# Two norms in a row in four stages of a perceiver network: both scale factors from one pass of moments, the once-normed tokens written behind the twice-normed ones

## The chip, the cores and the metric

The kernel runs on one core of one Trainium2 chip. The metric is the device time of one execution in microseconds (us), and the time of a kernel is the median of several executions. The core has TensorE (PE in the rows; its weight loads are PEld), VectorE (DVE), ScalarE (ACT), GpSimd (POOL) and SyncE (SP), which issues nearly all DMAs (SPq is its queue). The engines run their own instruction streams and wait for each other through semaphores.

## What is computed

The reference is a network of twelve sub-layers over 8 x 64 tokens of 512 float32 features, each added to the residual `x`. Before each one `x` is normed without weights. Four of the sub-layers begin by norming their input once more:

```python
def _layernorm(x, axis=-1, eps=1e-05):
    m = jnp.mean(x, axis=axis, keepdims=True)
    v = jnp.var(x, axis=axis, keepdims=True)
    return (x - m) / jnp.sqrt(v + eps)
...
x = x + _L1_xattn_ref(_layernorm(x, axis=-1), ...)   # begins with a layer norm (eps 1e-5), weights pre_g, pre_b
x = x + _L1_attn_ref(_layernorm(x, axis=-1), ...)    # begins with an RMS norm (eps 1e-6), weight rms_w; adds its input at the end
x = x + _L2_attn_ref(_layernorm(x, axis=-1), ...)    # begins with a layer norm (eps 1e-5), weights ln1_g, ln1_b; adds its input
x = x + _L3_attn_ref(_layernorm(x, axis=-1), ...)    # begins with a layer norm (eps 1e-5), weights g1, beta1; adds its input
```

A token that has been normed once has mean 0 and variance v / (v + eps), v being its variance in `x`. A second norm divides by the root of v / (v + eps) + eps2, so that the product of both divisions is one division by the root of v + eps2 * (v + eps), that is of v * (1 + eps2) + eps * eps2. For a mean of 0 the mean square that an RMS norm uses is the variance.

## The kernel before

The program is one list of stages. A stage is a list of blocks: in each block every engine has its own code, and a block ends with a barrier of all engines, so nothing of the next block starts before all of this one's instructions are issued and the engines have met. A DMA that a block has issued can land later, in a later block; whoever needs its data waits for its semaphore.

The 512 tokens lie in SBUF as four tiles of 128 tokens x 512 features (`t` runs over them): `m.x` (x_tokens in the rows) is the residual, `m.y` (normed_tokens) the normed tokens. `m.yT` (normed_features) holds the normed tokens turned to features x tokens, as four chunks (`c`) of 128 x 512, as the matmuls want them.

`normalise` is one block:

- SyncE issues the loads given in `ahead` one after another (L161), from the start of the block.
- VectorE computes moments of the four tiles (BN_STATS, L201, then BN_AGGR, L204) and variance + eps (L211; for the RMS norm L207 to L209). GpSimd raises that to the power -0.5 (L230), for all 4 x 128 tokens in one instruction. VectorE then writes the four normed tiles (L217, RMS L215).
- If `dstT` is given, TensorE turns the tiles with 16 transposes (L239), of which the first four each wait for one tile. ScalarE takes the chunks 0 and 2 out of PSUM, multiplied by `scale` and with `bias` added (L186), VectorE chunks 1 and 3 (L194, for the RMS norm without bias L192). With `vectors` given both first wait until **all** loads sent with that signal have landed: the weights of the norm are among them, but so are the larger weights of the projection behind.

In the four stages two such blocks stand in a row. The first norms `m.x` into `m.y` without `dstT`. The second norms `m.y`, with `dstT`. In L1_xattn and L1_attn the loads are sent in the first block of the two; in L2_attn and L3_attn, where the second block is the beginning of `transformer_layer`, they are sent in the second. L2_attn calls `transformer_layer` twice, and its second layer has one norm there, of the layer's own `m.y`. Behind the second block comes `linear_features`, whose first matmuls (L281) start the projection. `m.y`, the once-normed tokens, is added again at the end of L1_attn and in the attention of both transformer stages; L1_xattn does not use it again.

Of the kernel before, what the change touches and what calls it, by code (L numbers as in the profile page):

```python
# [66 lines left out]
class Machine:  # L67


    def __init__(self, nc, ctx, d):  # L70
# [11 lines left out]
        self.den = self.sb("var_eps", [P, T])  # L82
        self.rstd = self.sb("rstd", [P, T])
        self.slot_x = nc.dram_tensor("slot_inputs", (SLOT_ROWS, D), F32, kind="Internal").ap()
        self.slot_y = nc.dram_tensor("slot_outputs", (SLOT_ROWS, D), F32, kind="Internal").ap()
# [85 lines left out]

def normalise(m, dst, src, eps, rms=False, dstT=None, scale=None, bias=None, ahead=None, vectors=None):

# [4 lines left out]
    with m.block() as block:  # L178
# [18 lines left out]
        @block.vector  # L197
        def _(dve):
            step = Chain(dve, summed)
            for t in range(T):  # L200
                ins = dve.bn_stats(m.stats[:, t, :], src[:, t, :])  # L201
            step(ins)
            for t in range(T):
                ins = dve.bn_aggr(m.mv[:, t, :], m.stats[:, t, :])  # L204
            step(ins)
            if rms:
                step(dve.tensor_tensor(m.den[:], m.mv[:, :, 0], m.mv[:, :, 0], ALU.mult))  # L207
                step(dve.tensor_tensor(m.den[:], m.den[:], m.mv[:, :, 1], ALU.add))
                dve.tensor_scalar(m.den[:], m.den[:], eps, None, ALU.add).then_inc(*ready.up())  # L209
            else:  # L210
                dve.tensor_scalar(m.den[:], m.mv[:, :, 1], eps, None, ALU.add).then_inc(*ready.up())  # L211
            dve.wait_ge(*rooted.at(1))
            for t in range(T):
                if rms:
                    ins = dve.tensor_scalar(dst[:, t, :], src[:, t, :], m.rstd[:, t:t + 1], None, ALU.mult)  # L215
                else:
                    ins = dve.tensor_scalar(dst[:, t, :], src[:, t, :], m.mv[:, t, 0:1], m.rstd[:, t:t + 1],  # L217
                                            ALU.subtract, ALU.mult)
                if dstT is not None:
                    ins.then_inc(*normed.up())  # L220
            if dstT is not None:
                if landed:
                    dve.wait_ge(*landed)
                for c in range(1, C, 2):
                    take(dve, c)

        @block.gpsimd
        def _(pool):
            pool.wait_ge(*ready.at(1))
            pool.tensor_tensor(m.rstd[:], m.den[:], m.minus_half[:], ALU.pow).then_inc(*rooted.up())  # L230

        if dstT is not None:
# [1262 lines left out]
def L1_xattn(m):  # L1495
# [3 lines left out]
    with m.local(qT=[P, C, N], oT=[P, C, N], w=[P, C, D], pre=[P, 2, C], ln=[P, 2, C], rows=[P, 2, D],  # L1499
                 wkb=[P, C, D], wvb=[P, C, D], ctxT=[P, 2, C, SK]) as (qT, oT, w, pre, ln, rows, wkb, wvb, ctxT):  # L1500
        normalise(m, m.y, m.x, 1e-5, ahead=(
             vectors, (pre[:, 0, :], d["L1_xattn_pre_g"]), (pre[:, 1, :], d["L1_xattn_pre_b"]),
             (ln[:, 0, :], d["L1_xattn_ln_g"]), (ln[:, 1, :], d["L1_xattn_ln_b"]),
             (rows[:, 0, :], d["L1_xattn_ln_g_row"].partition_broadcast(P)),
             (rows[:, 1, :], d["L1_xattn_ln_b_row"].partition_broadcast(P)), (w[:], d["L1_xattn_Wq"])))
        normalise(m, m.y, m.y, 1e-5, dstT=m.yT, scale=pre[:, 0, :], bias=pre[:, 1, :], vectors=vectors)
        linear_features(m, [(qT, None, w, m.yT, None, ACT.Identity)], sent=vectors,
# [338 lines left out]

def transformer_layer(m, z, n, ln1, wq, bq, wk, bk, wv, bv, wo, bo, ln2, w1, b1, w2, b2, act, allowed=None, rope=None):

# [4 lines left out]
    with m.local(wa=[P, C, FF], wb=[P, FF // P, D], cols2=[P, 2, C], b1c=[P, FF // P], b2r=[P, D]) as \  # L1853
            (wa, wb, cols2, b1c, b2r):
        with m.local(qT=[P, C, N], kT=[P, C, N], wqo=[P, C, D], wkk=[P, C, D], cols=[P, 6, C],
# [3 lines left out]
            wvv = wb[:, 0:C, :]  # L1859
            normalise(m, n, z, 1e-5, dstT=m.yT, scale=cols[:, 0, :], bias=cols[:, 1, :], vectors=q_sent, ahead=(  # L1860
                q_sent, *[(cols[:, i, :], d[a]) for i, a in enumerate((ln1[0], ln1[1], bq, bk))],
# [77 lines left out]
def L3_attn(m):  # L1939
    normalise(m, m.y, m.x, 1e-5)  # L1940
    g = lambda a: f"L3_attn_{a}"
    with m.local(n=[P, T, D]) as (n,):
        transformer_layer(m, m.y, n, (g("g1"), g("beta1")), g("Wq"), g("bq"), g("Wk"), g("bk"), g("Wv"), g("bv"),
                          g("Wo"), g("bo"), (g("g2"), g("beta2")), g("W1"), g("b1"), g("W2"), g("b2"), ACT.Relu, rope=True)
    add_into(m, m.x, m.x, m.y)
# [426 lines left out]
def L1_attn(m):  # L2372
# [5 lines left out]
    with m.local(pairs=[P, 6, NC, N], va=[P, NC, N], u=[P, NC, N], W=[P, NC, 512], vecs=[P, 8, NC], convw=[P, NC, 4],  # L2378
# [627 lines left out]
```

## Time and profile before

| | |
|---|---|
| median of 3 runs | 4082.79 us (4082.26 to 4084.75) |
| the profiled execution, its own time | 4083.16 us |
| its span in the trace | 4081.4 us |
| TensorE busy | 3317.2 us, 81% of the span |
| VectorE busy | 1285.6 us, 31% |
| ScalarE busy | 730.7 us, 18% |
| GpSimd busy | 137.4 us, 3% |
| mean granted TensorE clock | 0.88 of full speed |

The shares are an average over stages with different limits. The four pairs of norms are short stretches, about 17 us each from the first moments to the first matmul, and in each TensorE stands idle for most of the time. In the timeline rows below a line is one run of equal instructions: start, duration, engine, line, operation, output<-inputs, shape, count, and in brackets how long the engine had been idle before it and what released it.

### The profile page before, as it was taken

What the parts mean: (1) busy time and instruction counts of PE and PEld (TensorE: products, weight loads), DVE (VectorE), ACT (ScalarE), POOL (GpSimd) and SP (SyncE); (2) the same over time, 40 slices, a digit from 0 to 9 for tenths busy, and PEclk for the clock granted to TensorE, in tenths of its full rate; (3) what the DMA queues carried; (4) which work ended last, traced back from release to release, by engine and by line L of the source; (5) the groups of instructions that cost most, each with busy time, mean ns of one, the idle gap of its engine ahead of it and who ended that gap; (6) DMA issues with size and microseconds to landing.
All of it is one profiled execution on the core that took longest, in us unless ns stands there. A gap on an engine that the chain in (4) does not pass through costs nothing. (4 is left out here: it accounts for less than half of the span.)

```text
span 4081.4 us, 42876 instructions
## 1 busy us (share of the span) xinstructions
PE 3317.2 (81%) x16360; PEld 1483.3 (36%) x16360; DVE 1285.6 (31%) x2692; ACT 730.7 (18%) x1187; POOL 137.4 (3%) x141
## 2 busy tenths in 40 slices
PE   7997799966997966679768979698997897667767
PEld 3443433322444422234324444333443443111111
DVE  2554410003445278644423030412444312000001
ACT  2442111001332210010001011011442111122111
POOL 0000010000000021000000000000000100000000
PEclk9997899987998977889888999799998998777776
DMA  3100289982110101121332030494000206999996
GB/s 124 39 28 32 93 341 414 416 333 98 52 62 21 56 21 52 52 83 52 126 119 96 0 133 0 161 413 160 30 31 18 107 11 255 421 421 420 420 420 288
DMA packets 93807, 654.91 MB, mean 160 GB/s; under 512 B 17779, under 2 KB 18548, under 8 KB 29940
## 3 DMA queue, kind: packets, MB, share of 16 engines
q1 hardware_dynamic: 89524, 639.56, 38.9%
q0 software_dynamic: 4160, 13.63, 0.9%
q8 instruction: 87, 1.43, 0.1%
q14 instruction: 36, 0.29, 0.0%
HBM read 643.71 MB, written 9.44 MB: 160 GB/s over the span
## 5 line engine op out<-in xcount | busy, mean ns | idle before, releaser
L475 PE MATMUL banks<-wvb,ctxT 128*128 128x512 f32 x768 | 346.6, 596 | 0.0
L2288 PE MATMUL banks<-wb,h 128*32 128x512 f32 x1024 | 174.2, 797 | 86.3 <-DMA wb<-in_L_ffn_w 45.6
L2277 PE MATMUL banks<-wa,mine 128*32 128x512 f32 x1024 | 191.5, 863 | 61.3 <-DMA wa<-in_L_ffn_w 42.8
L471 PE MATMUL banks<-ctxT,wkb 128*128 128x512 f32 x512 | 230.9, 596 | 3.3 <-PEq L125 3.3
L475 PEld LDWEIGHTS banks<-wvb,ctxT 128*128 128x128 f32 x768 | 139.2, 190 | 162.5 <-issue 153.6
L1296 PE MATMUL banks<-ring,xT 128*64 128x512 f32 x736 | 168.0, 611 | 12.9 <-DMA ring<-in_L_ffn_Wu 7.7
L281 PE MATMUL banks<-normed_features,wa 128*128 128x512 f32 x384 | 170.9, 608 | 3.5 <-PEq L130 3.5
L331 PE MATMUL banks<-wb,h 128*128 128x512 f32 x384 | 165.5, 593 | 3.1 <-PEq L130 3.1
L693 DVE COPY prT<-banks 128x512 f32<-128x512 f32 x160 | 109.5, 685 | 129.8 <-PE banks L545 128.2
L239 PE MATMUL banks<-identity,normed_tokens 128*128 128x128 f32 x160 | 42.9, 425 | 131.3 <-DVE normed_tokens L217 131.3
L593 ACT ACTIVATE pr<-pr,col 128x512 f32<-128x512 f32 x160 | 114.7, 717 | 119.4 <-DVE col L667 119.4
L471 PEld LDWEIGHTS banks<-ctxT,wkb 128*128 128x128 f32 x512 | 92.7, 190 | 111.0 <-issue 99.6
L545 PE MATMUL banks<-identity,pr 128*128 128x128 f32 x640 | 106.0, 291 | 21.6 <-ACT pr L587 8.0
L471 PE MATMUL banks<-extraT,wkb 128*128 128x512 f32 x256 | 116.4, 609 | 1.0 <-ACT extraT L581 1.0
L2692 PE MATMUL banks<-u,qw 128*128 128x512 f32 x192 | 85.2, 607 | 34.0 <-DMA qw<-in_L_attn_Q_W 34.0
L2584 PE MATMUL banks<-quantT,W 128*128 128x512 f32 x128 | 70.4, 702 | 52.2 <-PEq L130 27.7
L281 PEld LDWEIGHTS banks<-normed_features,wa 128*128 128x128 f32 x384 | 74.8, 196 | 98.2 <-issue 98.2
L545 PEld LDWEIGHTS banks<-identity,pr 128*128 128x128 f32 x640 | 78.3, 147 | 85.9 <-issue 59.5
L331 PEld LDWEIGHTS banks<-wb,h 128*128 128x128 f32 x384 | 72.7, 190 | 95.9 <-issue 95.9
L587 ACT ACTIVATE pr<-sc,col 128x512 f32<-128x512 f32 x96 | 69.3, 722 | 197.3 <-DVE col L662 197.3
L1296 PEld LDWEIGHTS banks<-ring,xT 128*64 128x64 f32 x736 | 62.0, 140 | 116.1 <-issue 114.8
L2288 PEld LDWEIGHTS banks<-wb,h 128*32 128x32 f32 x1024 | 29.1, 128 | 205.0 <-DMA wb<-in_L_ffn_w 131.5
(498 smaller groups left out, 4388.1 us busy)
## 6 DMA issues: line engine op xcount, KB each, us to landing
wa<-in_L_ffn_w SPq DMA_DIRECT2D x128, 1024.0 KB, 26.4
wb<-in_L_ffn_w SPq DMA_DIRECT2D x128, 1024.0 KB, 27.6
ring<-in_L_ffn_Wd SPq DMA_DIRECT2D x24, 2048.0 KB, 25.0
ring<-in_L_ffn_Wg SPq DMA_DIRECT2D x23, 2048.0 KB, 18.1
ring<-in_L_ffn_Wu SPq DMA_DIRECT2D x23, 2048.0 KB, 20.0
wa<-in_L_ffn_W SPq DMA_DIRECT2D x32, 1024.0 KB, 12.2
wb<-in_L_ffn_W SPq DMA_DIRECT2D x32, 1024.0 KB, 10.0
ctxT<-in_ctxT SPq DMA_DIRECT2D x24, 1024.0 KB, 4.8
```

What stands on the lines that cost most here:

```text
L281: ins = pe.matmul(m.ps[:, n % 4, :], buf[:, k, mm * P:(mm + 1) * P], srcT[:, k, :], start=(k == 0), stop=(k == kchunks - 1))
L331: ins = pe.matmul(m.ps[:, t, :], srcT[:, k, t * P:(t + 1) * P], buf[:, k, :], start=(k == 0), stop=(k == kchunks - 1))
L471: ins = pe.matmul(ps[:, u % 2, :], wkb[:, k, u * P:(u + 1) * P], (extraT if knorm else ctxT[:, par])[:, k, :], start=(k == 0), stop=(k == ...
L475: ins = pe.matmul(ps[:, u % 2, :], ctxT[:, par, k, r * P:(r + 1) * P], wvb[:, k, :], start=(k == 0), stop=(k == C - 1))
L545: ins = pe.transpose(ps[:, TB[j % 2], k * P:(k + 1) * P], pr[:, j % R, k * P:(k + 1) * P], m.ident[:])
L593: act.activation(pr[:, j % R, :], pr[:, j % R, :], ACT.Copy, scale=col[:, par, j, 3:4])\
L693: dve.tensor_copy(prT[:, j % RP, :, :], ps[:, TB[j % 2], :].rearrange("p (k n) -> p k n", k=KC))\
L1296: ins = pe.matmul(ps[H * side:H * side + H, 2 * kind + half, :], xT[:, p % 2, k, H * own:H * own + H], rows_of(where[(name, slot)], C)[:, ...
L2277: ins = pe.matmul(ps[B4 * q:B4 * q + B4, 0, :], mine[:, odd, k, :], wa[:, odd, k, q * 512:(q + 1) * 512], start=(k == 0), stop=(k == C - 1))
L2288: ins = pe.matmul(ps[B4 * q:B4 * q + B4, 2, :], h[:, Q * n + q, :], wb[:, odd, n, q, :], start=(n == 0), stop=(n == Q - 1))
L2584: return pe.matmul(ps[:, bank, :], sel[:, q % 4, c, :], quantT[:, q // 4, :], start=True, stop=True)
L2692: ins = pe.matmul(ps[:, n % 2 if n < NC else 2 + n - NC, :], qw[:, n % 2, k, :], u[:, k, :], start=(k == 0), stop=(k == NC - 1))
```

## The change

`normalise` gets two new arguments. With `again` (the eps of the second norm) the factor is computed from one pass of moments for both norms together, so the block writes the twice-normed tokens straight from `m.x`. With `once` it also computes the factor of the first norm alone (`den_once`, and a second power on GpSimd into `rstd_once`) and writes the once-normed tokens into that buffer, behind the other four tiles on VectorE and ahead of VectorE's chunks 1 and 3. The first block of each pair goes. L1_xattn gets `again` alone; L1_attn, L3_attn and the first layer of L2_attn get both.

```diff
+def normalise(m, dst, src, eps, dstT=None, scale=None, bias=None, ahead=None, vectors=None, again=None, once=None):
...
-            if rms:
-                step(dve.tensor_tensor(m.den[:], m.mv[:, :, 0], m.mv[:, :, 0], ALU.mult))
-                step(dve.tensor_tensor(m.den[:], m.den[:], m.mv[:, :, 1], ALU.add))
-                dve.tensor_scalar(m.den[:], m.den[:], eps, None, ALU.add).then_inc(*ready.up())
+            if again is not None:
+                dve.tensor_scalar(m.den[:], m.mv[:, :, 1], 1.0 + again, eps * again, ALU.mult, ALU.add).then_inc(*ready.up())
             else:
                 dve.tensor_scalar(m.den[:], m.mv[:, :, 1], eps, None, ALU.add).then_inc(*ready.up())
+            if once is not None:
+                dve.tensor_scalar(m.den_once[:], m.mv[:, :, 1], eps, None, ALU.add).then_inc(*ready.up())
             dve.wait_ge(*rooted.at(1))
             for t in range(T):
...
+                ins = dve.tensor_scalar(dst[:, t, :], src[:, t, :], m.mv[:, t, 0:1], m.rstd[:, t:t + 1],
+                                        ALU.subtract, ALU.mult)
                 if dstT is not None:
                     ins.then_inc(*normed.up())
+            if once is not None:
+                dve.wait_ge(*rooted.at(2))
+                for t in range(T):
+                    dve.tensor_scalar(once[:, t, :], src[:, t, :], m.mv[:, t, 0:1], m.rstd_once[:, t:t + 1],
+                                      ALU.subtract, ALU.mult)
             if dstT is not None:
                 if landed:
                     dve.wait_ge(*landed)
...
         def _(pool):
             pool.wait_ge(*ready.at(1))
             pool.tensor_tensor(m.rstd[:], m.den[:], m.minus_half[:], ALU.pow).then_inc(*rooted.up())
+            if once is not None:
+                pool.wait_ge(*ready.at(2))
+                pool.wait_ge(*rooted.at(1))
+                pool.tensor_tensor(m.rstd_once[:], m.den_once[:], m.minus_half[:], ALU.pow).then_inc(*rooted.up())
...
-        normalise(m, m.y, m.x, 1e-5, ahead=(
+        normalise(m, m.y, m.x, 1e-5, again=1e-5, dstT=m.yT, scale=pre[:, 0, :], bias=pre[:, 1, :], vectors=vectors, ahead=(
...
-        normalise(m, m.y, m.y, 1e-5, dstT=m.yT, scale=pre[:, 0, :], bias=pre[:, 1, :], vectors=vectors)
...
-            normalise(m, n, z, 1e-5, dstT=m.yT, scale=cols[:, 0, :], bias=cols[:, 1, :], vectors=q_sent, ahead=(
+            twice = {} if before is None else {"again": 1e-5, "once": z}
+            normalise(m, n, z if before is None else before, 1e-5, **twice, dstT=m.yT, scale=cols[:, 0, :], bias=cols[:, 1, :],
+                      vectors=q_sent, ahead=(
...
 def L2_attn(m):
-    normalise(m, m.y, m.x, 1e-5)
...
-                              allowed="strided")
+                              allowed="strided", before=None if i else m.x)
...
 def L3_attn(m):
-    normalise(m, m.y, m.x, 1e-5)
...
-        normalise(m, m.y, m.x, 1e-5, ahead=(
+        normalise(m, rms_normed, m.x, 1e-5, again=1e-6, once=m.y, dstT=m.yT, scale=rmsw[:], vectors=vectors, ahead=(
...
-        normalise(m, rms_normed, m.y, 1e-6, rms=True, dstT=m.yT, scale=rmsw[:], vectors=vectors)
```

On VectorE the start of L1_attn reads so before (`pairs` holds the RMS-normed tokens, L130 is the end of a block):

```order
L201 BN_STATS stats<-x_tokens 128x6 x4
L204 BN_AGGR mean_var<-stats 128x2 x4
L211 TENSOR_SCALAR var_eps<-mean_var 128x4
L217 TENSOR_SCALAR normed_tokens<-x_tokens,mean_var,rstd 128x512 x4
L130 UNCONDITIONAL_BRANCH
L197 UNCONDITIONAL_BRANCH
L201 BN_STATS stats<-normed_tokens 128x6 x4
L204 BN_AGGR mean_var<-stats 128x2 x4
L207 TENSOR_TENSOR var_eps<-mean_var 128x4
L208 TENSOR_TENSOR var_eps<-var_eps,mean_var 128x4
L209 TENSOR_SCALAR var_eps<-var_eps 128x4
L215 TENSOR_SCALAR pairs<-normed_tokens,rstd 128x512 x4
L192 TENSOR_SCALAR normed_features<-banks,rmsw 128x512 x2
```

And so with the change, at the same place on VectorE:

```order
L207 BN_STATS stats<-x_tokens 128x6 x4
L210 BN_AGGR mean_var<-stats 128x2 x4
L213 TENSOR_SCALAR var_eps<-mean_var 128x4
L217 TENSOR_SCALAR var_eps_once<-mean_var 128x4
L220 TENSOR_SCALAR pairs<-x_tokens,mean_var,rstd 128x512 x4
L227 TENSOR_SCALAR normed_tokens<-x_tokens,mean_var,rstd_once 128x512 x4
L198 TENSOR_SCALAR normed_features<-banks,rmsw 128x512 x2
```

One set of moments and one barrier are gone, the writing of normed_tokens stands behind that of pairs instead of ahead of it, and it now stands between pairs and the two chunks that VectorE takes from PSUM.

On GpSimd the start of L2_attn reads so before (L740 is the first instruction of the attention's own block):

```order
L130 UNCONDITIONAL_BRANCH
L227 UNCONDITIONAL_BRANCH
L230 TENSOR_TENSOR rstd<-var_eps,minus_half 128x4
L130 UNCONDITIONAL_BRANCH
L227 UNCONDITIONAL_BRANCH
L230 TENSOR_TENSOR rstd<-var_eps,minus_half 128x4
L130 UNCONDITIONAL_BRANCH
L737 UNCONDITIONAL_BRANCH
L740 MEMSET v 128x64
```

With the change:

```order
L132 UNCONDITIONAL_BRANCH
L235 UNCONDITIONAL_BRANCH
L238 TENSOR_TENSOR rstd<-var_eps,minus_half 128x4
L242 TENSOR_TENSOR rstd_once<-var_eps_once,minus_half 128x4
L132 UNCONDITIONAL_BRANCH
L749 UNCONDITIONAL_BRANCH
L752 MEMSET v 128x64
```

The number of powers stays at two, but the second now stands in the same block and runs while VectorE writes tiles; before, VectorE waited during both.

## Rows read from the trace of the kernel before

**Rows 1.** Timeline at the start of L1_xattn.

```profile
920.99 2.47 DVE L201 BATCH_NORM_STATS2 stats<-x_tokens 128x6 f32<-128x512 f32 x4 [0.55 <-PEq L130]
...
923.70 0.43 SPq L161 DMA_DIRECT2D w<-in_L_xattn_Wq  x1
...
927.47 2.47 DVE L201 BATCH_NORM_STATS2 stats<-normed_tokens 128x6 f32<-128x512 f32 x4 [0.30 <-PEq L130]
...
934.23 0.78 ACT L186 ACTIVATE normed_features<-banks,pre 128x512 f32<-128x512 f32 x1 [33.69 <-PE banks L239]
...
937.84 10.35 PE L281 MATMUL banks<-normed_features,w 128*128 128x512 f32 x19 [1.15 <-PEq L130]
```

**Rows 2.** Timeline at the start of L1_attn.

```profile
1313.98 2.47 DVE L201 BATCH_NORM_STATS2 stats<-x_tokens 128x6 f32<-128x512 f32 x4 [0.30 <-PEq L130]
...
1317.77 0.47 SPq L161 DMA_DIRECT2D convw<-in_L_attn_conv_w  x1
...
1320.41 2.47 DVE L201 BATCH_NORM_STATS2 stats<-normed_tokens 128x6 f32<-128x512 f32 x4 [0.30 <-PEq L130]
...
1327.32 0.69 ACT L186 ACTIVATE normed_features<-banks,rmsw 128x512 f32<-128x512 f32 x1 [14.43 <-PE banks L239]
...
1330.87 14.39 PE L281 MATMUL banks<-normed_features,W 128*128 128x512 f32 x29 [1.09 <-PEq L130]
```

**Rows 3.** Timeline at the start of L2_attn.

```profile
2114.88 2.47 DVE L201 BATCH_NORM_STATS2 stats<-x_tokens 128x6 f32<-128x512 f32 x4 [0.30 <-PEq L130]
...
2121.31 2.47 DVE L201 BATCH_NORM_STATS2 stats<-normed_tokens 128x6 f32<-128x512 f32 x4 [0.30 <-PEq L130]
...
2125.52 1.92 DVE L217 TENSOR_SCALAR n<-normed_tokens,mean_var,rstd 128x512 f32<-128x512 f32 x4 [1.12 <-POOL rstd L230]
...
2126.12 4.03 PE L239 MATMUL banks<-identity,n 128*128 128x128 f32 x16 [12.27 <-DVE n L217]
...
2129.61 1.53 DVE L194 TENSOR_SCALAR normed_features<-banks,cols 128x512 f32<-128x512 f32 x2 [2.17 <-DMA bound<-in_strided]
...
2131.44 13.97 PE L281 MATMUL banks<-normed_features,wqo 128*128 128x512 f32 x32 [1.29 <-PEq L130]
```

**Rows 4.** Timeline at the start of L3_attn.

```profile
3146.72 2.47 DVE L201 BATCH_NORM_STATS2 stats<-x_tokens 128x6 f32<-128x512 f32 x4 [0.30 <-PEq L130]
...
3153.14 2.47 DVE L201 BATCH_NORM_STATS2 stats<-normed_tokens 128x6 f32<-128x512 f32 x4 [0.30 <-PEq L130]
...
3157.96 4.41 PE L239 MATMUL banks<-identity,n 128*128 128x128 f32 x16 [12.27 <-DVE n L217]
...
3162.03 1.53 DVE L194 TENSOR_SCALAR normed_features<-banks,cols 128x512 f32<-128x512 f32 x2 [2.75 <-DMA trig<-in_rope_trig]
...
3163.86 11.38 PE L281 MATMUL banks<-normed_features,wqo 128*128 128x512 f32 x22 [1.49 <-PEq L130]
```

**Rows 5.** DMA issues: size, and us from issue to landing.

```profile
w<-in_L_xattn_Wq SPq DMA_DIRECT2D x1, 1024.0 KB, 7.2
...
convw<-in_L_attn_conv_w SPq DMA_DIRECT2D x1, 16.0 KB, 5.8
```

**Rows 6.** Timeline of L3_attn's rotation: GpSimd beside VectorE, then VectorE alone.

```profile
3200.46 5.83 POOL L1902 TENSOR_TENSOR kT<-kT,trig 128x512 f32<-128x512 f32 x4
3202.12 5.33 DVE L1913 TENSOR_TENSOR qT<-qT,tmp 128x512 f32<-128x512 f32 x4
3207.37 1.28 DVE L1913 TENSOR_TENSOR kT<-kT,tmp 128x512 f32<-128x512 f32 x2
```

**Rows 7.** Windows: us, busy time per engine, granted clock, DMA share, GB/s.

```profile
940.00:942.00 2.00, 2.00 (x3) 0.69 (x3) 0.00 (x0) 0.00 (x0) 0.00 (x0) 0.55 1.01 426
...
1334.00:1336.00 2.00, 2.00 (x5) 0.76 (x4) 0.00 (x0) 0.00 (x0) 0.00 (x0) 0.92 1.00 426
2128.00:2130.00 2.00, 2.00 (x12) 1.91 (x10) 0.39 (x1) 0.40 (x1) 0.00 (x0) 0.59 0.49 166
3166.00:3168.00 2.00, 2.00 (x4) 0.75 (x4) 0.00 (x0) 0.00 (x0) 0.00 (x0) 0.68 1.02 430
```

More of the change, by code:

```diff
@@ L83, in __init__ @@
         self.rstd = self.sb("rstd", [P, T])
+        self.den_once = self.sb("var_eps_once", [P, T])
+        self.rstd_once = self.sb("rstd_once", [P, T])
         self.slot_x = nc.dram_tensor("slot_inputs", (SLOT_ROWS, D), F32, kind="Internal").ap()
@@ L169, in _ @@
             start_loads(sp, ahead)
-def normalise(m, dst, src, eps, rms=False, dstT=None, scale=None, bias=None, ahead=None, vectors=None):
+def normalise(m, dst, src, eps, dstT=None, scale=None, bias=None, ahead=None, vectors=None, again=None, once=None):
     summed, ready, rooted = m.sig("moments_step"), m.sig("variance_ready"), m.sig("rstd_ready")
@@ L205, in _ @@
             step(ins)
-            if rms:
-                step(dve.tensor_tensor(m.den[:], m.mv[:, :, 0], m.mv[:, :, 0], ALU.mult))
-                step(dve.tensor_tensor(m.den[:], m.den[:], m.mv[:, :, 1], ALU.add))
-                dve.tensor_scalar(m.den[:], m.den[:], eps, None, ALU.add).then_inc(*ready.up())
+            if again is not None:
+                dve.tensor_scalar(m.den[:], m.mv[:, :, 1], 1.0 + again, eps * again, ALU.mult, ALU.add).then_inc(*ready.up())
             else:
                 dve.tensor_scalar(m.den[:], m.mv[:, :, 1], eps, None, ALU.add).then_inc(*ready.up())
+            if once is not None:
+                dve.tensor_scalar(m.den_once[:], m.mv[:, :, 1], eps, None, ALU.add).then_inc(*ready.up())
             dve.wait_ge(*rooted.at(1))
             for t in range(T):
[L214 to L218, printed above, removed]
+                ins = dve.tensor_scalar(dst[:, t, :], src[:, t, :], m.mv[:, t, 0:1], m.rstd[:, t:t + 1],
+                                        ALU.subtract, ALU.mult)
                 if dstT is not None:
                     ins.then_inc(*normed.up())
+            if once is not None:
[3 more added lines that the diff above has]
+                                      ALU.subtract, ALU.mult)
             if dstT is not None:
@@ L1844, in L2_xattn, with transformer_layer @@
         linear_tokens(m, m.x, m.yT, None, w, C, bv[:], m.x, sent=vectors)
-def transformer_layer(m, z, n, ln1, wq, bq, wk, bk, wv, bv, wo, bo, ln2, w1, b1, w2, b2, act, allowed=None, rope=None):
+def transformer_layer(m, z, n, ln1, wq, bq, wk, bk, wv, bv, wo, bo, ln2, w1, b1, w2, b2, act, allowed=None, before=None, rope=None):
     d = m.d
@@ L1943, in L3_attn @@
         transformer_layer(m, m.y, n, (g("g1"), g("beta1")), g("Wq"), g("bq"), g("Wk"), g("bk"), g("Wv"), g("bv"),
-                          g("Wo"), g("bo"), (g("g2"), g("beta2")), g("W1"), g("b1"), g("W2"), g("b2"), ACT.Relu, rope=True)
+                          g("Wo"), g("bo"), (g("g2"), g("beta2")), g("W1"), g("b1"), g("W2"), g("b2"), ACT.Relu, rope=True,
+                          before=m.x)
     add_into(m, m.x, m.x, m.y)
```

## The prediction, made before the changed kernel ran

> **What bounds the kernel now.** I read the page first: TensorE is busy 81% of the span and no other engine over 31% (table above), so time is won where TensorE stands idle. The timeline of the four places that the change touches comes next. In each the reader should see the same chain: moments, variance, a wait for GpSimd's power, four tiles, a barrier, then all of it once more, then transposes, chunks taken out of PSUM, a barrier, the first matmul of the projection. TensorE has nothing to do from the end of the stage before to the transposes; in L2_attn that is 12.27 us of idleness [rows 3]. From the first moments to the first matmul it is 937.84 - 920.99 = 16.85 us in L1_xattn, 16.89 in L1_attn, 16.56 in L2_attn and 17.14 in L3_attn [rows 1 to 4].
>
> The third view is what releases the chunks. In L1_xattn and L1_attn ScalarE's first chunk waits for TensorE [rows 1, 2]; in L2_attn and L3_attn VectorE's chunks wait for a DMA, the last small load of the list (bound, trig) [rows 3, 4]. So the pairs are of two kinds. Where the loads were sent in the first of two blocks they have time to land behind the second norm; where they are sent in the second they already end last. The change treats the kinds differently, and this is where the sum is decided.
>
> **L2_attn and L3_attn.** What goes is the first block entire: from first moments to first moments 2121.31 - 2114.88 = 6.43 us and 3153.14 - 3146.72 = 6.42 us [rows 3, 4]. The loads are at the start of the block that stays, so they move ahead by the same time, and the stretch behind them stays as long as it is: in L2_attn chunks at +8.30 us after the moments began, first matmul at +10.13; in L3_attn +8.89 and +10.72. No load of the stage was sent in the block that goes, so nothing loses cover.
>
> What is added on VectorE must end before the chunks. The fused tiles start at 2125.52 - 2121.31 = +4.21 and take 1.92 us, to +6.13; the four once-normed tiles have the same form, another 1.92, to +8.05, say +8.1 with the semaphore. The DMA lands at +8.30 in L2_attn: hidden with 0.2 us to spare. In L3_attn 0.8 us are spare. The new variance (4 columns) lies in VectorE's 1.12 us wait for the power. The second power starts when the first has ended, at about +4.2, and by that same wait takes at most 1.1: ready at +5.3, 0.8 ahead of the fused tiles' end. If the landing were no cover, the added tiles would cost 1.9 us in a stage.
>
> One small loss in L2_attn: its 16 transposes took 4.03 us because the clock rose inside them (0.59 in a window that would read 0.50 at half clock [rows 7]); those of L3_attn took 4.41 [rows 4]. Started at +4.81, 4.41 would end them at +9.22, against VectorE's second chunk at +9.07. I take 0.2 us as lost. Sum: 6.43 - 0.2 + 6.42 = 12.65 us.
>
> **L1_xattn.** Here `ahead` stays in the block that stays, so the loads do not move, while the norm is ready earlier. ScalarE's first chunk came 934.23 - 927.47 = 6.76 us after the second moments began; from 920.99 that is 927.75. But the weight w, last of the list, is issued at 923.70 and lands 7.2 us later, at 930.90 [rows 1, 5]. Both engines wait for all loads, so the chunks start at 930.9: the landing that was hidden behind the second norm now ends last, and eats 3.15 us. From there to the first matmul I take the stretch of L2_attn, where chunks also waited for a DMA: 2131.44 - 2129.61 = 1.83 us. First matmul at 932.73 instead of 937.84: 5.1 us.
>
> **L1_attn.** The last load, convw, is issued at 1317.77 and lands 5.8 us later, at 1323.57 [rows 2, 5]. The norm alone would allow the first chunk at 1313.98 + (1327.32 - 1320.41) = 1320.89, and earlier by the two small VectorE steps that the RMS norm no longer has. The landing ends last again, 2.7 us late. First matmul at 1323.57 + 1.83 = 1325.40 instead of 1330.87: 5.45 us. The once-normed tiles end at about 1313.98 + 8.1 = 1322.1, 1.5 us ahead of the landing: free. They are read again only in the last block of the stage.
>
> **The second power beside VectorE.** Before, VectorE waited during every power. Now one runs while VectorE writes tiles. The trace shows that the two can slow each other: four of VectorE's additions took 5.33 us beside GpSimd's products, 1.33 each, and two more took 1.28 without, 0.64 each [rows 6]. Those are whole tiles; the power has 4 columns. From below the price is nothing. From above one engine waits out the other: VectorE's fused tiles, and the transposes with them, up to 1.0 us late, which costs 1.0 in L2_attn, about 0.6 in L3_attn (chunks there have 0.4 to spare), and some 0.3 in L1_attn; or the power is held until the fused tiles end at +6.13 and the once-normed tiles run from +7.2 to +9.1, 0.8 late in L2_attn and 0.2 in L3_attn. I take nothing, since the one instruction is small against the rows that show the slowing, and keep 2 us for the range.
>
> The Trainium skill speaks against me here: "SBUF — State Buffer", section "Who interferes with whom", has VectorE's tensor_scalar among the operations that can take the port pair shared with GpSimd, for a whole instruction, the other engine blocking fully. By that rule the held power is the case, and the sum would be 1.0 us smaller. Rows 6 agree that the two engines wait for each other, but show it for additions of two inputs.
>
> **The clock.** The granted clock is half (1.2 GHz) when the transposes begin, and what it costs is the matmuls at half clock behind them. In the window from 940 it reads 0.55, that is 0.2 of 2 us at full clock: it rose at 941.8, 3.96 us after the first matmul. In the same way 1334.32 in L1_attn, 3.45 after, and 3167.28 in L3_attn, 3.42 after; in L2_attn it rose at 2129.64, before the first matmul [rows 7]. A matmul that waits for nothing takes twice as long at half clock, so these 10.8 us cost 5.4. The change moves the moments of all four, and makes the pause between transposes and matmuls longer by 1 to 1.5 us in the two L1 stages. I take no change. The bounds: all four as L2_attn gives 5.4 us back; L2_attn like the others and one more such delay in the two L1 stages costs 1.7 + 2 x 1.8 = 5.3.
>
> **The sum.** 5.1 + 5.45 + 12.65 = 23.2 us. Against the profiled execution, 4083.16 - 23.2 = 4059.96; that execution lies 0.37 us above the median of the runs shown, so the median is forecast at 4059.8. Nothing behind the four places gives it back: all loads of later blocks are issued behind the barriers, by an SP queue that moves with them. Even the stages that stream weights begin to do so only at their own start.
>
> **The rivals.**
> 1. *The landing is no bound in the L1 stages*, because the loads there land sooner once nothing else has changed places: full savings of 6.48 and 6.43 + 0.33 us. The sum is 12.65 + 13.2 = 25.9, time 4056.9. For it: the load w took 7.2 us, and nothing says that it must. Against: the loads of the list, their order and their moment are the same.
> 2. *The added work on VectorE and GpSimd is exposed*, by the power that collides or by 1.9 us of tiles that miss their cover in L2_attn and L3_attn: 1 to 3 us back, time 4061 to 4063. For it: a margin of only 0.2 us in L2_attn, and rows 6. Against: the landing is late in all three places with `once`.
> 3. *The change saves nothing of note*, since later DMA-bound stages end when their transfers do: time 4082. This needs loads that are already under way when the norms run. Against it: in the four timelines no load of a later block stands ahead of the norms, and the loads of rows 1 to 4 all belong to their own block.
> 4. *Slower.* One mechanism could do it: a clock that stays at half. Each us of matmuls at half clock costs 0.5, so with 23.2 us won, 46 us more at half clock would be needed, 11.6 in each of four stages, before it decides, and 63 us for a time 0.2% above before (4091). The longest rise seen behind these norms is 3.96 us, so the projection would have to run at half clock nearly whole. Time then 4083 to 4091.
>
> **How the numbers follow.** My forecast with its small errors (4057.5 to 4062) gets 0.65, the first rival 0.08, the second 0.17, the third 0.04, the slow one 0.02, and 0.04 is left for another clock outcome (4055 to 4066). 0.2% of the time is 8.2 us, about what a measurement of this kernel can tell from no change. The range from 4055 to 4066 takes in the power's 2 us above, the clock's 5.3 us on one side and most of it on the other, and leaves out the last two rivals. Faster has 0.94, same 0.04, slower 0.02.
>
> **What would show it.** In the changed profile the stretch from first moments to first matmul should read about 11.7 us in L1_xattn, 11.4 in L1_attn, 10.3 in L2_attn and 10.7 in L3_attn, with the chunks released by a DMA in all four. The power for rstd_once should last 1.0 us and the once-normed tiles should start right behind the fused ones; a gap there, or fused tiles over 0.5 us apart, shows the collision. If the chunks in the L1 stages wait for TensorE, the landing was misjudged. If the four stretches are as forecast and the time is not, it went into the clock or a later stage. A landing much later than 7.2 and 5.8 us after the issue, or once-normed tiles that end behind it, would make the prediction wrong by its size, not by its sign.

## The result, and the profile after

The changed kernel's median is 4058.7 us over four runs (4054.47 to 4062.64), against 4082.53 us over four runs of the kernel before (4078.19 to 4084.75). The ratio is 0.9941, 95% interval 0.9926 to 0.9955. The forecast was 4059.8. The profiled execution took 4062.64 us, 20.5 less than the profiled one before. It is one of the two longer of the four runs: two took 4054.5 and 4055.0 us, two took 4062.4 and 4062.6.

First the page of the changed kernel. TensorE's busy time is that of before (table above: 3317.2 us), VectorE's is 15 us less, which lay in the stretches in which TensorE stood idle. The gain is idle time of TensorE:

```profile
span 4060.9 us, 42817 instructions
...
PE 3319.8 (82%) x16360; PEld 1486.3 (37%) x16360; DVE 1270.9 (31%) x2653; ACT 730.5 (18%) x1187; POOL 137.8 (3%) x140
```

The timeline of the changed kernel at the start of L1_xattn, which answers to [rows 1]:

```profile
923.63 2.47 DVE L207 BATCH_NORM_STATS2 stats<-x_tokens 128x6 f32<-128x512 f32 x4 [0.55 <-PEq L132]
...
924.91 1.35 SPq L163 DMA_DIRECT2D ln<-in_L_xattn_ln_b  x1
...
927.26 0.43 SPq L163 DMA_DIRECT2D w<-in_L_xattn_Wq  x1
...
928.49 4.41 PE L251 MATMUL banks<-identity,normed_tokens 128*128 128x128 f32 x16 [25.96 <-DVE normed_tokens L220]
934.48 1.45 ACT L192 ACTIVATE normed_features<-banks,pre 128x512 f32<-128x512 f32 x2 [31.31 <-DMA w<-in_L_xattn_Wq]
...
936.31 4.61 PE L293 MATMUL banks<-normed_features,w 128*128 128x512 f32 x5 [3.41 <-PEq L132]
```

ScalarE's chunks are no longer released by TensorE but by the landing of w, as forecast, and both of its chunks now run in one row, since the transposes were done 1.6 us before. The stretch from moments to matmul is 12.68 us.

The start of L2_attn in the changed kernel, which answers to [rows 3]:

```profile
2109.35 2.47 DVE L207 BATCH_NORM_STATS2 stats<-x_tokens 128x6 f32<-128x512 f32 x4 [0.30 <-PEq L132]
...
2112.51 1.01 POOL L238 TENSOR_TENSOR rstd<-var_eps,minus_half 128x4 f32<-128x4 f32 x1 [117.19 <-DVE var_eps_once L217]
...
2113.56 1.92 DVE L220 TENSOR_SCALAR n<-x_tokens,mean_var,rstd 128x512 f32<-128x512 f32 x4 [1.05 <-POOL rstd L238]
2113.67 1.39 POOL L242 TENSOR_TENSOR rstd_once<-var_eps_once,minus_half 128x4 f32<-128x4 f32 x1
2114.16 4.41 PE L251 MATMUL banks<-identity,n 128*128 128x128 f32 x16 [5.84 <-DVE n L220]
2115.39 1.92 DVE L227 TENSOR_SCALAR normed_tokens<-x_tokens,mean_var,rstd_once 128x512 f32<-128x512 f32 x4
2117.70 1.45 ACT L192 ACTIVATE normed_features<-banks,cols 128x512 f32<-128x512 f32 x2 [23.66 <-DMA bound<-in_strided]
2117.70 1.72 DVE L200 TENSOR_SCALAR normed_features<-banks,cols 128x512 f32<-128x512 f32 x2 [0.39 <-DMA bound<-in_strided]
...
2119.72 1.19 PE L293 MATMUL banks<-normed_features,wqo 128*128 128x512 f32 x1 [1.15 <-PEq L132]
```

The once-normed tiles end at +7.96 us, VectorE idles 0.39 us, and the load lands at +8.35. The cover of the forecast (+8.05 against +8.30) is there, and as thin. The second power takes 1.39 us beside the tiles, where the first took 1.01 with VectorE waiting; it still ends 0.33 us ahead of the tiles that need it, and the fused tiles keep their 1.92 us. In L1_attn and L3_attn the rows are alike, with the landing at +9.45 and +9.18.

Put side by side, in us, with the four stretches from first moments to first matmul:

| | L1_xattn | L1_attn | L2_attn | L3_attn | sum |
|---|---|---|---|---|---|
| before | 16.85 | 16.89 | 16.56 | 17.14 | 67.44 |
| forecast | 11.74 | 11.42 | 10.33 | 10.72 | 44.2 |
| changed kernel | 12.68 | 11.16 | 10.37 | 11.01 | 45.22 |

The four places save 22.2 us. The spans differ by 20.5, so 1.7 us went elsewhere: the first of the four places began 2.64 us later than before (923.63 against 920.99), although nothing ahead of it had changed, and the rest of the program gave 0.9 back. No run shows why; in the ten profiles without idle products that place begins anywhere from 915.75 to 923.63 us.

### The profile page after: what moved, and what is told of

It is laid out like the page before. It is cut to its first block and busy times, and to the rows that moved or that the text cites. A ratio compares the mean times of both kernels' runs of the same rounds, so it can differ in the third digit from the quotient of the medians.

```text
span 4060.9 us, 42817 instructions
## 1 busy us (share of the span) xinstructions
PE 3319.8 (82%) x16360; PEld 1486.3 (37%) x16360; DVE 1270.9 (31%) x2653; ACT 730.5 (18%) x1187; POOL 137.8 (3%) x140
```

## The experiments

### The change in the two L1 stages alone, and in the two transformer stages alone

```diff
 def L2_attn(m):
+    normalise(m, m.y, m.x, 1e-5)
...
-                              allowed="strided", before=None if i else m.x)
+                              allowed="strided")
```

(the same in L3_attn), and for the other half the calls of L1_xattn and L1_attn put back as they were.

> The change in L1_xattn and L1_attn alone; L2_attn and L3_attn as before. My theory (the savings of the four places are independent, and in the two L1 stages the landing of the loads ends last): the stretch from first moments to first matmul is 11.7 to 12.7 us in L1_xattn and 11.2 to 11.4 in L1_attn (16.85 and 16.89 before), and 16.6 and 17.1 in L2_attn and L3_attn as before; the time 9.5 to 10.5 us under before, ratio 0.9975. Rival (the gain is found mostly in these two stages, because the later ones give it back): the time falls by 15 us or more, ratio 0.996 or less.

> The change in L2_attn and L3_attn alone; L1_xattn and L1_attn as before, with their two norms each. Theory: stretches of 10.4 us in L2_attn and 10.7 to 11.0 in L3_attn, 16.85 and 16.89 in the L1 stages; the time 12 to 12.6 us under before, ratio 0.997. Rival (the second power and the tiles written behind are on the path): stretches of 12.3 and 12.9.

Measured: the L1 stages alone 4075.44 us against 4083.67, ratio 0.997 (0.9959 to 0.9982), 8.2 us; the transformer stages alone 4067.87, ratio 0.9961 (0.9948 to 0.9975), 15.8 us. The stretches repeat far better than the times (each is read from one profile; the unchanged ones differ by up to 0.3 us from those of the kernel before): 12.58 and 11.37 us in the first kernel's changed stages (16.88 and 17.21 in the others), 10.38 and 10.56 in the second's (16.85 and 16.88 in the others). By stretches the halves save 9.8 and 12.8 us, by medians 8.2 and 15.8, in sum 24.0, against 23.8 for the whole change. So both expectations of the time were missed (9.5 to 10.5 and 12 to 12.6), while the stretches came as expected within 0.3 us. The misses are smaller than the scatter of single runs: the first kernel's ten runs reach from 4061.39 to 4077.44, and 18 of the kernel before from 4076.83 to 4090.36. The rival that the L1 half carries most of it falls. By the stretches the gains are independent and add up (22.6 us for the halves, 22.2 for the whole); the times agree with that and are too coarse to show it.

### Four more tiles on VectorE

```diff
             if once is not None:
                 dve.wait_ge(*rooted.at(2))
+                for t in range(T):
+                    dve.tensor_scalar(m.spare[:, t, :], src[:, t, :], m.mv[:, t, 0:1], m.rstd_once[:, t:t + 1],
+                                      ALU.subtract, ALU.mult)
```

> The whole change, and in L1_attn, L2_attn and L3_attn four more tiles of the same form are written (into a spare buffer) ahead of the once-normed ones, 1.88 us of VectorE each time. Theory (the once-normed tiles are covered by the landing, which came 8.35, 9.18 and 9.45 us after the moments began in L2_attn, L3_attn and L1_attn, against 7.95 for the end of the tiles): VectorE is ready at 9.84, so its chunks come 1.5 us later in L2_attn, 0.7 in L3_attn and 0.4 in L1_attn, 2.6 us in all against the changed kernel. Rival (no cover, the tiles already cost what they last): 1.9 us in each, 5.6 in all. Second rival (the tiles are nowhere near the path): 0.

Measured: the median is 4065.72 us, ratio 0.9957 (0.994 to 0.9973). The timeline at L2_attn, in the kernel with eight tiles:

```profile
2104.72 2.47 DVE L208 BATCH_NORM_STATS2 stats<-x_tokens 128x6 f32<-128x512 f32 x4 [0.30 <-PEq L133]
...
2112.58 1.91 DVE L231 TENSOR_SCALAR normed_tokens<-x_tokens,mean_var,rstd_once 128x512 f32<-128x512 f32 x4
2113.12 1.45 ACT L193 ACTIVATE normed_features<-banks,cols 128x512 f32<-128x512 f32 x2 [25.41 <-DMA bound<-in_strided]
2114.41 1.52 DVE L201 TENSOR_SCALAR normed_features<-banks,cols 128x512 f32<-128x512 f32 x2
...
2116.23 2.04 PE L297 MATMUL banks<-normed_features,wqo 128*128 128x512 f32 x2 [2.30 <-PEq L133]
```

VectorE's chunks begin at +9.69, with no wait in brackets: it is late itself now, while ScalarE still waits for the load. The stretch is 11.51 us, 1.14 over the changed kernel; in L3_attn 11.52, 0.51 more, in L1_attn 11.41, 0.25 more. That is 1.9 us for 5.6 us of added work. The order (most where the cover was thinnest) is the theory's, the size is three quarters of it. VectorE was ready at +9.70 and not at +9.84, and in L2_attn its second chunk no longer waited for the transposes (1.52 us for two chunks instead of 1.72). L1_attn says little here, since its landing itself came later, at +9.66 instead of +9.45:

```profile
1317.07 1.27 ACT L193 ACTIVATE normed_features<-banks,rmsw 128x512 f32<-128x512 f32 x2 [10.75 <-DMA convw<-in_L_attn_conv_w]
```

The four tiles of the change itself are thus free, and in L2_attn and L3_attn the next four are not. The median lies 7.0 us above that of the changed kernel, far more than the 1.9 us of the stretches and still less than the spread of its four runs (8.2 us).

### Both factors from one power

```diff
-            pool.wait_ge(*ready.at(1))
-            pool.tensor_tensor(m.rstd[:], m.den[:], m.minus_half[:], ALU.pow).then_inc(*rooted.up())
-            if once is not None:
-                pool.wait_ge(*ready.at(2))
-                pool.wait_ge(*rooted.at(1))
-                pool.tensor_tensor(m.rstd_once[:], m.den_once[:], m.minus_half[:], ALU.pow).then_inc(*rooted.up())
+            pool.wait_ge(*ready.at(1))
+            n = T if once is None else 2 * T
+            pool.tensor_tensor(m.rstd2[:, 0:n], m.den2[:, 0:n], m.minus_half[:, 0:n], ALU.pow).then_inc(*rooted.up())
```

> The whole change, but both factors come from one GpSimd instruction of 8 columns instead of two of 4, so no power runs beside VectorE's tiles. In the changed kernel the second power took 1.39 us beside them, against 1.01 alone. Theory (the slowed power is hidden behind the fused tiles): the stretches stay within 0.2 us of the changed kernel's (L2_attn 10.4, L3_attn 10.7 to 11.0, L1_attn 11.2), provided that 8 columns last about 1.1 us. Rival (the power's cost goes by its columns): it lasts 2 us, the fused tiles start 1 us later, the transposes end 1 us later, and L2_attn reads 11.4, L3_attn 11.4, L1_attn 11.6.

Measured: 4059.47 us, ratio 0.9943 (0.9927 to 0.996), the same as the changed kernel. In the view of this line of the kernel with one power, the longest is that of 8 columns:

```profile
L240 POOL TENSOR_TENSOR rstd<-var_eps,minus_half x18: 1005/1007/1637, 19.2 to 3372.9; 128x4 f32<-128x4 f32 x15, 128x8 f32<-128x8 f32 x3
```

8 columns last 1.64 us against 1.01 for 4, so my condition (about 1.1) did not hold: the power goes partly by its columns. The transposes begin at +5.52 instead of +4.81, and L2_attn reads 11.07 us, 0.70 more. In L3_attn it is 11.07 too, only 0.06 more, since the landing at +9.18 had been as late. L1_attn reads 11.51, near the rival's 11.6, but for another reason: its chunks still wait for convw, which landed at +9.79 here instead of +9.45. The two powers are the better form: the second one lies under the fused tiles even at 1.39 us.

### A signal of its own for the norm's weights

```diff
-        normalise(m, m.y, m.x, 1e-5, again=1e-5, dstT=m.yT, scale=pre[:, 0, :], bias=pre[:, 1, :], vectors=vectors, ahead=(
-             vectors, (pre[:, 0, :], d["L1_xattn_pre_g"]), (pre[:, 1, :], d["L1_xattn_pre_b"]),
+        normalise(m, m.y, m.x, 1e-5, again=1e-5, dstT=m.yT, scale=pre[:, 0, :], bias=pre[:, 1, :], vectors=own, ahead=[(
+             own, (pre[:, 0, :], d["L1_xattn_pre_g"]), (pre[:, 1, :], d["L1_xattn_pre_b"])),
+             (vectors, (ln[:, 0, :], d["L1_xattn_ln_g"]), (ln[:, 1, :], d["L1_xattn_ln_b"]),
```

and likewise in L1_attn (rmsw) and in `transformer_layer` (cols 0 and 1).

> The whole change, and the norm's own weights get a signal of their own, sent first: the chunks wait for these alone, and the landing of the projection's weights is waited for by the first matmul. The order of the loads is the same. Theory (the landing ends last in all four, and holds back the chunks): the chunks no longer wait for a DMA. First moments to first matmul: L1_xattn at the landing of w, 9.9 to 10.9 us instead of 11.7 to 12.7; L1_attn 10.4 instead of 11.2, L3_attn 10.4 instead of 11.0, bound by the transposes' end at 9.2; L2_attn 10.4 as it is. All in all 3 us less than the changed kernel. Rival (the chunks are bound by the transposes at half clock anyway): nothing changes but in L1_xattn.

Measured: 4055.12 us, ratio 0.9924 (0.9911 to 0.9937). The start of L1_xattn in that kernel:

```profile
915.75 2.47 DVE L207 BATCH_NORM_STATS2 stats<-x_tokens 128x6 f32<-128x512 f32 x4 [0.55 <-PEq L132]
...
922.55 0.78 ACT L192 ACTIVATE normed_features<-banks,pre 128x512 f32<-128x512 f32 x1 [26.81 <-PE banks L251]
...
926.72 2.08 PE L293 MATMUL banks<-normed_features,w 128*128 128x512 f32 x2 [1.72 <-DMA w<-in_L_xattn_Wq]
```

The first chunk starts at +6.80, released by TensorE, and the wait for w has moved to the first matmul, at +10.97. The other stretches are 10.32, 10.37 and 10.37 us. In sum 42.03, against 45.22: the 3 us that were expected, in the places that were expected (L1_xattn a little above its range of 9.9 to 10.9).

### The loads that the projection does not need, sent later

```diff
-             (ln[:, 0, :], d["L1_xattn_ln_g"]), (ln[:, 1, :], d["L1_xattn_ln_b"]),
-             (rows[:, 0, :], d["L1_xattn_ln_g_row"].partition_broadcast(P)),
-             (rows[:, 1, :], d["L1_xattn_ln_b_row"].partition_broadcast(P)), (w[:], d["L1_xattn_Wq"])))
+             (w[:], d["L1_xattn_Wq"])))
...
+             (late, (ln[:, 0, :], d["L1_xattn_ln_g"]), (ln[:, 1, :], d["L1_xattn_ln_b"]),
+              (rows[:, 0, :], d["L1_xattn_ln_g_row"].partition_broadcast(P)),
+              (rows[:, 1, :], d["L1_xattn_ln_b_row"].partition_broadcast(P)))])
```

The added lines are the end of the list that `linear_features` sends; in L1_attn the four `vecs` and `convw` behind K0. Their later users, L1_xattn's second norm and L1_attn's convolution, now wait for the new signal.

> The whole change, and in L1_xattn and L1_attn the loads that the first projection does not need (in L1_xattn the four of the second norm, in L1_attn four vectors and convw) are sent in the next block, behind its own loads, under a signal of their own. The chunks still wait for all that is sent with the norm. Theory (the landing of the last load binds, and it is late because of what stands ahead of it): the last load lands about 6.4 us after the block begins in L1_xattn and 8.1 in L1_attn, the transposes end last there, and the stretches read 10.4 in both instead of 11.7 to 12.7 and 11.2: 2 to 3 us less in all. Rival (w lands when it does, whatever stands ahead): no change in L1_xattn.

Measured: 4050.9 us, ratio 0.9917 (0.9904 to 0.9929). The start of L1_xattn there:

```profile
921.17 2.47 DVE L207 BATCH_NORM_STATS2 stats<-x_tokens 128x6 f32<-128x512 f32 x4 [0.54 <-PEq L132]
...
929.25 1.45 ACT L192 ACTIVATE normed_features<-banks,pre 128x512 f32<-128x512 f32 x2 [28.71 <-DMA w<-in_L_xattn_Wq]
929.26 0.81 DVE L200 TENSOR_SCALAR normed_features<-banks,pre 128x512 f32<-128x512 f32 x1 [1.91 <-DMA w<-in_L_xattn_Wq]
930.47 0.81 DVE L200 TENSOR_SCALAR normed_features<-banks,pre 128x512 f32<-128x512 f32 x1 [0.41 <-PE banks L251]
931.59 2.05 PE L293 MATMUL banks<-normed_features,w 128*128 128x512 f32 x2 [1.15 <-PEq L132]
```

w was issued 2.81 us earlier (+0.82 instead of +3.63) and landed 2.77 us earlier, at +8.08 instead of +10.85. I had said 6.4, with the 5 us under way that such a load takes in L2_attn; here it is 7.26, as it was with four more loads ahead of it. ScalarE's first chunk waits for it still, but VectorE's last chunk is released by the transposes, so the stretch is 10.42 us. In L1_attn the last load landed at +8.57 (8.1 expected) and the stretch is 10.30. This and the last experiment together show that what stood in L1_xattn's and L1_attn's way was the landing of the list.

### Both of these, and both with the one power

> The whole change, with a signal for the norm's own weights, the later loads in the next block, and both factors from one power. Theory: no chunk waits for a DMA, all four stretches read 10.3 to 10.5 us, 41.6 in sum against 45.2 in the changed kernel's profile, so 3 to 4 us less than the changed kernel; the spread of the runs (8 us among the changed kernel's four) hides most of it in the time. Rival (the earlier matmuls come at half clock for longer and give it back): stretches as said, but the time from the first matmul to the next stage is longer by the same amount.

> The changed kernel with both the norm's own signal and the later loads, and with its two powers of 4 columns. It takes the power of 8 columns (1.64 us, exposed by 0.7 us in three stages) out of the kernel that had all three. Theory: stretches from first moments to first matmul of 10.4 in L1_xattn and 10.3 to 10.4 in the other three, 41.5 in sum, against 43.6 with the one power and 45.2 in the changed kernel. The time 3 to 4 us under the changed kernel's typical 4058.7, but single runs differ by more than that. Rival (the power of 8 columns is not what kept the stretches at 11.0): 11.0 in the last three here too.

The two are the unions of the edits above. Measured: with the one power 4058.93 us, ratio 0.9934 (0.9921 to 0.9947), stretches 10.42, 11.00, 11.07, 11.07; with two powers 4053.42 us, ratio 0.9923 (0.9909 to 0.9937), stretches 10.41, 10.31, 10.37, 10.37, in sum 41.46. The first missed its expectation in three stages by the 8-column power, and its median is that of the changed kernel in spite of 1.7 us less in the stretches; the second met its own in the stretches, and its median is 5.3 us lower where 3 to 4 were expected. Against the kernel with later loads alone (42.08 in sum, 4050.9 us) the last 0.6 us of stretches can't be seen in the time.

### TensorE kept busy ahead of the transposes

Here nothing is computed that is used: TensorE multiplies the identity with itself into a free bank. The kernel is that of the last experiment (two powers, the own signal, the later loads), with this edit:

```diff
             def _(pe):
+                for n, after in ((10, None), (6, summed.at(1)), (2, rooted.at(1))):
+                    if after:
+                        pe.wait_ge(*after)
+                    for i in range(n):
+                        pe.matmul(m.ps[:, 7, 0:P], m.ident[:], m.ident[:], start=True, stop=True)
                 for c in range(C):
```

> The kernel with the own signal and the later loads, and in every norm that is turned TensorE does 18 idle products of the identity with itself (128x128, into a bank that nobody reads) ahead of the transposes: 10 from the start of the block, 6 when the moments' first step is done, 2 when the power is done. They leave the result alone. Theory (behind each norm the first matmuls run at half clock only because TensorE stood idle): the granted clock stays full through the norm, the 16 transposes end about 1 us sooner (in the rows of before a transpose took 0.27 us at full clock against 0.42), the stretch falls to 9 to 9.6 us, and the half-clock matmuls behind go, 3 to 6 us each time. Per norm 2 to 2.5 us, and with some 20 norms that are turned the time falls by 20 to 45 us. Rival (18 small products are too few, or the clock falls in spite of them): the stretches stay at 10.4 and the time within 3 us of the kernel without them. Second rival (the idle products are in the transposes' way): stretches longer than 10.4.

Measured: 4023.97 us, ratio 0.9857 (0.9839 to 0.9875), and 29.5 us under the same kernel without the idle products. The windows over L3_attn's norm in the kernel without them (the column before DMA's is the granted clock):

```profile
3128.00:3130.00 2.00, 0.00 (x0) 0.00 (x0) 1.37 (x8) 0.00 (x0) 0.55 (x1) 0.94 0.50 64
3130.00:3132.00 2.00, 0.91 (x2) 0.37 (x2) 1.51 (x4) 0.00 (x0) 1.85 (x2) 0.50 0.91 377
3132.00:3134.00 2.00, 2.00 (x9) 1.72 (x9) 2.00 (x5) 0.78 (x1) 0.00 (x0) 0.50 0.82 322
...
3138.00:3140.00 2.00, 2.00 (x3) 0.67 (x2) 0.00 (x0) 0.00 (x0) 0.00 (x0) 0.50 0.79 328
```

and with them:

```profile
3103.00:3105.00 2.00, 1.94 (x18) 1.75 (x17) 1.97 (x7) 0.00 (x0) 0.00 (x0) 1.00 0.15 8
3105.00:3107.00 2.00, 1.90 (x16) 1.71 (x15) 0.91 (x6) 0.00 (x0) 1.44 (x2) 1.00 0.81 242
3107.00:3109.00 2.00, 1.61 (x10) 0.99 (x9) 2.00 (x6) 0.14 (x1) 0.95 (x1) 1.00 0.97 394
...
3111.00:3113.00 2.00, 1.06 (x3) 0.61 (x4) 0.64 (x1) 0.00 (x0) 0.00 (x0) 1.00 0.24 37
```

The clock stays full through the norm and the pause behind it, here as in L1_attn and L2_attn. In L1_xattn, where TensorE had stood idle for 21 us before the first product, it reads 0.50 from 914 to 918, rises between 918 and 920 and is full at the first matmul. The groups of transposes, before and here:

```profile
L239 PE MATMUL banks<-identity,normed_tokens 128*128 128x128 f32 x160 | 42.9, 425 | 131.3 <-DVE normed_tokens L217 131.3
```

```profile
L256 PE MATMUL banks<-identity,normed_tokens 128*128 128x128 f32 x160 | 22.9, 280 | 2.0
```

A transpose takes 280 ns in place of 425. The stretches fall to 9.78, 9.58, 9.69 and 9.70 us, mostly a little above the 9 to 9.6 expected, and the first matmuls behind all four run at full clock. In the last three the bound has moved to the once-normed tiles, as in L2_attn:

```profile
2094.48 1.91 DVE L227 TENSOR_SCALAR normed_tokens<-x_tokens,mean_var,rstd_once 128x512 f32<-128x512 f32 x4
2095.05 1.58 ACT L192 ACTIVATE normed_features<-banks,cols 128x512 f32<-128x512 f32 x2 [23.62 <-PE banks L256]
2096.30 1.52 DVE L200 TENSOR_SCALAR normed_features<-banks,cols 128x512 f32<-128x512 f32 x2
```

VectorE takes its chunks right behind these tiles, without a wait, while ScalarE is done first: the tiles that were free under a late landing are so no longer. 17 norms are turned in this kernel, so it is 1.7 us each, a little under the 2 to 2.5 I expected. Of all versions tried this one is the fastest, 1.4% under the kernel before.

## Why the prediction was right

**The two kinds of pairs** were what decided the sum, and held. In L2_attn the whole first block came off (stretch 10.37 us, forecast 10.33, the 0.2 us for colder transposes included: they took 4.41 us, in two rows of VectorE's chunks 1.72 instead of 1.53). In the two L1 stages the landing took the norm's place as the end, and the two experiments on the loads removed it from there. The sum of the stretches came out 1.0 us short of the forecast (22.2 us won, 23.2 forecast), nearly all of it in L1_xattn.

**L1_xattn** was the term mis-sized: 4.17 us won instead of 5.1. w did land 7.2 us after its issue, as before, but the issue came at +3.63 and not +2.71, because the issue of ln_b ahead of it lasted 1.35 us where the others last 0.43. The view of DMA queues shows a fetch of instructions (q8) at just that time, in the changed kernel between 923 and 928:

```profile
q1 hardware_dynamic: 630, 0.12, 12.6%
q8 instruction: 1, 0.02, 1.2%
```

and none in the kernel before from 920 to 925. The other profiles agree. In the L1 stages alone, the eight tiles, the one power, the own signal, and signal and later loads with two powers, one SP issue of this block lasts 1.52 to 1.91 us with a fetch beside it; in the kernel with this stage as before none does, and the fetch comes 8.8 us after the moments began (9.0 in the kernel before), when SP has long issued its list. In the three others with the later loads (with one power, without the own signal, with idle products) the fetch begins 0.24 to 0.82 us after the start of the last issue, which lasts 0.42 us as ever. So a fetch beside an issue need not lengthen that issue: in the lengthened ones it begins at most 0.18 us after their start, or up to 0.23 us ahead of it. I take it that the shorter program moved a fetch from where SP had nothing to issue into the middle of its list. No experiment moved the fetch alone, so this is argued from eleven profiles and not shown.

**L1_attn** won 5.73 us, forecast 5.45, with convw issued at +3.61 against +3.79 and again 5.8 us under way. **L3_attn** won 6.13, forecast 6.42: trig landed at +9.18 against +8.89.

**The second power** was priced at nothing, with 2 us in the range. It took 1.39 us where the first took 1.01, and was hidden. That VectorE's tiles are what lengthened it is likely and not shown: no run has the second power without tiles beside it. The Trainium skill, "SBUF — State Buffer", section "Who interferes with whom", has the blocking last for one instruction, and one tile takes 0.48 us, so the extra 0.38 us is within it. That the power would be held through all four tiles, at 1.0 us of lost time, was my reading and not the page's, and the trace refutes it. The rows that I priced it from were misread too: only three of VectorE's four additions in [rows 6] ran beside GpSimd, about 1.55 us each, and the fourth started when GpSimd had ended (3206.29) and took 0.68:

```profile
3206.77 0.68 DVE L1913 TENSOR_TENSOR qT<-qT,tmp 128x512 f32<-128x512 f32 x1
```

The slowing there is larger than I said, and the price of nothing rested on the power's small size alone.

**The clock** was taken as unchanged, with bounds of 5.4 us either way. In the profile of the changed kernel it cost more than before:

```profile
940.00:942.00 2.00, 2.00 (x4) 0.80 (x3) 0.00 (x0) 0.00 (x0) 0.00 (x0) 0.57 1.01 426
...
1330.00:1332.00 2.00, 2.00 (x5) 0.89 (x4) 0.00 (x0) 0.40 (x1) 0.00 (x0) 0.79 0.81 344
...
2122.00:2124.00 2.00, 2.00 (x5) 0.86 (x4) 0.00 (x0) 0.00 (x0) 0.00 (x0) 0.82 0.99 414
...
3145.00:3147.00 2.00, 2.00 (x4) 0.82 (x3) 0.00 (x0) 0.00 (x0) 0.00 (x0) 0.57 0.71 274
```

Read as [rows 7] were: the rise comes 5.4, 5.9, 3.0 and 2.8 us after the first matmul, 17.1 us in sum against 10.8, so 3.1 us dearer. L2_attn, which had been spared before, pays now, and the two L1 stages pay more. This was the term mis-sized most, and it looks like chance in the main: in the kernel with the own signal, L2_attn has the same stretch of 10.37 us, its first matmul comes at 2107.51, and the window from 2107 reads 0.99 already:

```profile
2107.00:2109.00 2.00, 1.49 (x4) 0.80 (x5) 0.21 (x1) 0.00 (x0) 0.00 (x0) 0.99 0.51 66
```

The pause ahead of the matmuls, which the prediction names, does not order the delays: in the changed kernel TensorE pauses 1.95 us in L1_attn and 1.80 in L3_attn, and the clock rises 5.9 and 2.8 us after the first matmul. In the kernel with one power it pauses 1.60 us in L1_attn, its first matmul there comes at 1318.96, and the clock is full:

```profile
1319.00:1321.00 2.00, 2.00 (x5) 0.98 (x6) 0.00 (x0) 0.00 (x0) 0.00 (x0) 1.00 0.67 139
```

Over the ten profiles without idle products the time at half clock, read in the 8 us behind the first matmul, is 0 in eight of the 40 places and up to 6.1 us in the others. What decides it is not shown, beyond that with idle products it was 0 in all four places.

**The total** came out 1.1 us above the measured median, which is luck as well as working. Two terms were too favourable, 0.9 us in L1_xattn and 3.1 us of clock in the profile, and the median does not show either. One run of this program differs from the next by up to 8 us (4054.47 and 4062.64 in the changed kernel), so an agreement within 1 us says little. What was forecast and can be checked is the four stretches, 44.2 us in sum, measured 45.22.

**The rivals.** The first (no landing in the way) is refuted by the rows. The second (added work exposed) is refuted for the change as made, though in L2_attn only 0.39 us of idle VectorE stood between it and the facts; with idle products ahead of the transposes the added tiles are exposed. The third (given back later) is refuted by the measured ratio, and both halves keep their gain. The slow one did not come near.

## What to carry to other kernels

When a change takes compute out of a stretch that also hides a transfer, price it by the landing of the last load that shares the signal, not by the compute removed; and see which loads share it, since a signal that covers more than its waiter needs is the next bound. Work added to an engine is free only up to that landing: a doubled dose, or a landing that no longer binds, exposes it. Read a gain of 20 us in 4 ms from the stretches of the profile, because single executions of one kernel scattered by 8 to 16 us; and where TensorE idles before a chain of matmuls, try idle products first, which won more here (29.5 us) than the change under study.

## What the runs showed of the hardware

- A power on GpSimd over 128 x 4 float32 took 1.01 us, over 128 x 8 it took 1.64 us, and 1.39 us over 128 x 4 when it ran beside VectorE's tile operations, which kept their 1.92 us for four.
- In six profiles an SP issue that started at most 0.18 us before a fetch of instructions, or up to 0.23 us after the fetch began, lasted 1.35 to 1.91 us instead of 0.43. In two others a fetch that began 0.24 and 0.34 us into an issue left it at 0.42. The fetch lay at +8.8 to +9.0 us in the two kernels with L1_xattn as before and at +0.9 to +1.6 in the others.
- With idle products ahead of the transposes the granted clock read 1.00 at the first matmuls of the four stages, and in three of them through the norm too; in L3_attn it had read 0.50 in the same places without them; the mean granted clock of the whole run went from 0.883 to 0.901.
- The first touched place began between 915.75 and 923.63 us in ten profiles of kernels whose programs do the same work up to there (that of the idle products left out). Times of single executions scatter by as much.
